# The third block of a normalised x: turned over by DMA in place of TensorE

## The reference

```
h = relu(layernorm(x))                                   # 1250 x 1024
s = sigmoid(h @ wenc.T + benc)                           # 1250 x 500
agg = segment_sum((s @ conv_weight)[src] * edge_weight, dst)
x = x + (agg + s @ lin_weight.T) @ wdec.T + bdec
h = relu(layernorm(x))
x = x + D^-1/2 (A + I) D^-1/2 (h @ W.T + b)              # A counts the edges src -> dst
```

## Time and profile before

| | |
|---|---|
| median of three runs | 471.36 us |
| the profiled execution | 471.27 us |
| its span | 469.5 us |
| TensorE busy | 461.0 us (98%) |
| VectorE busy | 317.4 us (68%) |
| ScalarE busy | 207.8 us (44%) |
| GpSimd busy | 44.0 us (9%) |
| transposing DMAs into h16T | 8, issued from 48.3 to 71.6 us |

### The profile page before, as it was taken

The page is one execution under the profiler, slowest core; times in us unless marked ns, Lnnn a source line. Parts: engine busy times, 40 slices in busy tenths (PEclk is TensorE's granted clock), DMA queues, the critical chain, the costliest instruction groups (busy, mean ns, idle before and its releaser), DMA issues.

```text
span 469.5 us, 9232 instructions
## 1 busy us (share of the span) xinstructions
PE 461.0 (98%) x3456; PEld 400.5 (85%) x3456; DVE 317.4 (68%) x596; ACT 207.8 (44%) x412; POOL 44.0 (9%) x60
## 2 busy tenths in 40 slices
PE   6999999999999999999999999999999999999997
PEld 5999999978888888889888878888889988888886
DVE  5999997777857851594668786929542467566652
ACT  6986797645541141222444444547442522222220
POOL 3522110000000000000000000465500000000000
PEclk8899999999999999999999999999999999999999
DMA  8820848482224570538530005161959315546542
GB/s 308 259 82 23 156 85 217 129 312 77 68 68 84 113 246 0 114 109 341 201 121 1 0 1 209 62 265 51 372 220 391 140 36 235 202 179 224 192 168 104
DMA packets 46111, 72.35 MB, mean 154 GB/s; under 512 B 25292, under 2 KB 34142, under 8 KB 44402
## 3 DMA queue, kind: packets, MB, share of 16 engines
q1 hardware_dynamic: 45746, 71.34, 45.4%
q0 software_dynamic: 320, 0.39, 0.4%
HBM read 44.33 MB, written 22.01 MB: 141 GB/s over the span
## 4 chain that ended last, share of the span: by engine, by line
PE 79%; DVE 9%; DMA 6%; ACT 3%; issue 2%; POOL 1%; SPq 0%; POOLq 0%; DVEq 0%; ACTq 0%
PE bank L1408 18%; PE bank L1424 18%; PE bank L1409 18%; PE bank L1410 18%; DVE weighted L1328 3%; DMA row_scratch<-dis 2%; PE bank L1521 2%; DMA raw<-adj_scratch 2%; DVE stats L1049 1%; PE bank L1566 1%; PE bank L1541 1%; DMA dis_row<-row_scratch 1%; PE bank L1523 1%; PE bank L1525 1%; DMA h<-x 1%
## 5 line engine op out<-in xcount | busy, mean ns | idle before, releaser
L1424 PE MATMUL bank<-a,h_hi 128*128 128x256 f16 (+3 forms) x400 | 85.5, 270 | 0.0
L1424 PE MATMUL bank<-a,h_lo 128*128 128x256 f16 (+3 forms) x400 | 85.5, 270 | 0.0
L1408 PE MATMUL bank<-right,left 128*128 128x512 f32 (+1 forms) x148 | 56.1, 379 | 0.0
L1409 PE MATMUL bank<-right,left 128*128 128x512 f32 (+1 forms) x148 | 55.9, 378 | 0.0
L1410 PE MATMUL bank<-right,left 128*128 128x512 f32 (+1 forms) x148 | 55.9, 378 | 0.0
L1393 DVE SCALAR_TENSOR_TENSOR x<-bank,dis_u,x 128x512 f32<-128x512 f32 (+2 forms) x37 | 26.7, 722 | 35.9 <-PE bank L1410 35.8
L1013 ACT CAST left<-zs 128x512 fp32r<-128x512 f32 x35 | 21.6, 624 | 61.3 <-PE bank L1410 61.2
L1408 PE MATMUL bank<-unit,g 128*128 128x500 f32 (+3 forms) x120 | 42.4, 354 | 0.4 <-DVE unit L1265 0.4
L1424 PEld LDWEIGHTS bank<-a,h_hi 128*128 128x128 f16 (+1 forms) x400 | 39.0, 98 | 4.1 <-issue 0.3
L1424 PEld LDWEIGHTS bank<-a,h_lo 128*128 128x128 f16 (+1 forms) x400 | 39.1, 98 | 3.7
L1410 PE MATMUL bank<-unit,g 128*128 128x500 f32 (+3 forms) x120 | 42.3, 352 | 0.0
(11 more groups left out here) (162 smaller groups left out, 1114.2 us busy)
## 6 DMA issues: line engine op xcount, KB each, us to landing
right_scratch<-right SPq DMA_DIRECT2D x5, 2048.0 KB, 8.1
right<-right_scratch SPq DMA_DIRECT2D x5, 2048.0 KB, 7.6
whole<-w SPq DMA_DIRECT2D x7, 1024.0 KB, 7.7
adj_scratch<-stage SPq DMA_DIRECT2D x50, 125.0 KB, 2.3
raw<-adj_scratch SPq DMA_DIRECT2D x2, 2500.0 KB, 8.9
h<-x SPq DMA_DIRECT2D x9, 512.0 KB, 6.0
x<-x SPq DMA_DIRECT2D x9, 512.0 KB, 6.8
out<-x SPq DMA_DIRECT2D x18, 256.0 KB
```

The source lines that it names most:

```text
L1408: pe.matmul(o, lhs[0], rhs[0], start=first, stop=False, skip_group_check=True)
L1409: pe.matmul(o, lhs[0], rhs[1], start=False, stop=False, skip_group_check=True)
L1424: ins = pe.matmul(o, h1[i][0:n, k, 128 * f:128 * (f + 1)], moving, start=(k == 0 and part == 0 and i == 0), stop=(k == T - 1 and part == p ...
```

## The change

Block 2 is turned over by DMA too. With `BY_DMA = 2` every place that asks for it treats tiles 4 and 5 as tiles 6 to 9 were treated: the factor in the scale, two activations in norm 4 and norm 5, splits, transposing DMAs, the copies L896 and L1157, and the sigmoids' scale. The 16 transposes, L899 and L1159 of this block are gone. The splits and the DMAs of tiles 4 and 5 come behind e(1,0), the copies behind e(1,2), each quarter's low part right behind its high part, and norm 6 after them. The DMAs of block 2 wait for `edges`, as it is now the first such block; those of block 3 now wait for block 2 to be copied; norm 6 writes `x16` after tile 4's DMAs, and norm 7 after tile 5's. In the order written out, the windows and hots 2 and 3 fall between e(1,2) and the copies of block 2; before, all of block 2 stood ahead of them.

```diff
-BY_DMA = 3
+BY_DMA = 2
...
     third, fourth, fifth = statistics(2), statistics(3), statistics(4)
     beside = {
-        (1, 0): turn(2), (1, 1): fourth, (1, 2): [("norm", 6)], (1, 3): [("norm", 7), ("split", 6), ("turn", 6)],
+        (1, 0): [("split", 4), ("turn", 4), ("split", 5), ("turn", 5)], (1, 1): fourth, (1, 2): both(turn(2)) + [("norm", 6)],
+        (1, 3): [("norm", 7), ("split", 6), ("turn", 6)],
         (2, 0): [("split", 7), ("turn", 7)] + fifth[:1], (2, 1): fifth[1:], (2, 2): both(turn(3)) + [("norm", 8)],
```

## The result

The changed kernel took 475.71 us (median of six, 474.98 to 477.26) against 471.3 us (471.05 to 471.7): a ratio of 1.0094, with a 95% interval of 1.0083 to 1.0105. The kernel became slower by 4.4 us, as forecast.

A forecast was written before the change was run, and what follows sets the result against it. TensorE's order of work was taken as the bound, with any wait put before it paid in full. Terms 1.14 - 1.67 + 0.85 + 1.6 + 2.0 + 0.2 + 0.3 = +4.4 us on 471.27 gave 475.7, range 472.4 to 479.0.

The forecast's parts named there:

- e(1,0): TensorE's encoder product of block 1, feature group 0: forecast +1.14 us late, behind norm 4's added activation.
- window 0: First ("win", w) step, on TensorE in block 1's products: forecast 0.53 us ahead, with the transposes' 1.67 us gone.
- e(2,0): Encoder product of block 2, feature group 0: forecast +1.9 us late, held by hots, the DMA and the first copies.
- e(2,1): Encoder product of block 2, feature group 1: forecast +3.9 us late, another +2.0 from ScalarE's queue behind the wait.
- e(2,2): Encoder product of block 2, feature group 2: forecast +4.1 us late, starting at 57.55 against 53.46.
- window 12: Later ("win", w) step on TensorE, waiting for ScalarE's stage: forecast +4.4 us late, another +0.3 from GpSimd's scale.
- the walk: Step-by-step forecast along the engines' orders: 475.7 us, its own range 474.7 to 476.9, chance 0.60.
- the landing of the last transfer: Tile 5's second transposing DMA: issued at 42.8, forecast to land 3.6 us later, at 46.4.
- The last hold: Norm 8 on ScalarE waits for GpSimd's scale: forecast start between 65.1 and 66.1, +3.9 to +4.9 us.
- ScalarE did not swallow it: Rival: ScalarE's 4.5 us free in 27 to 41 absorb the added 2.28 us: 469.6 us, chance 0.06.
- The quick transfer: Rival: tile 5 lands by 43.8 and norm 6 starts 2.6 us earlier: +1.8, 473.1 us, chance 0.12.
- The clock: Rival: TensorE's idle waits bring its granted clock down, costing another +2.5 us: 478.2 us, chance 0.14.

The follow-up runs named there:

- run 4: Changed kernel with norm 4 moved behind e(0,2), the product of block 0, feature group 2: 474.21 us, ratio 1.0069.
- run 5: Changed kernel with norm 4 moved behind the product of block 0, feature group 2, and norm 5 behind the step edges: 472.85 us, ratio 1.0036.
- run 6: Changed kernel with norm 4 as in run 4 and the splits and DMAs of tiles 4 and 5 ahead of the step edges: 470.7 us, ratio 0.9991.
- run 7: Changed kernel with norm 6 ahead of the copies of block 2: 477.47 us, ratio 1.013.
- run 8: Kernel of run 6 with norms 6 to 9 each one product later: 469.99 us, ratio 0.9974.
- run 10: Kernel of run 8 with the statistics of tile 8 ahead of split 6 on VectorE: 469.78 us, ratio 0.9963.
- run 11: Changed kernel with the splits and DMAs of tiles 4 and 5 ahead of the step edges, norm 4 not moved: 472.3 us, ratio 1.0017.
- run 12: Kernel of run 11 with 12 matmuls that nobody reads put into the step edges: 471.01 us, ratio 1.0009.
- run 1: Kernel before, block 2 still turned by TensorE, but norms 4 and 5 also write x16 (two activations for one): 473.6 us, ratio 1.0052.
- run 2: Changed kernel with the four DMAs of tiles 4 and 5 as plain copies, block 2 not turned over: 475.15 us, ratio 1.0088.
- run 3: Changed kernel with norm 5 moved behind the step edges: 473.87 us, ratio 1.0049.

## Why the prediction was right

Point by point, TensorE behind its own times of before, with the 0.77 us of the later start taken off:

| step | forecast | measured |
|---|---|---|
| e(1,0), behind norm 4's pair | +1.1 | +1.1 (32.19) |
| window 0, less the transposes | -0.5 | -0.7 (40.82) |
| e(2,0), behind the DMA | +1.9 | +2.8 (49.12) |
| e(2,1), behind norm 6 | +3.9 | +4.5 (54.82) |
| e(2,2) | +4.1 | +4.7 (58.97) |
| window 12, behind GpSimd's scale | +4.4 | +5.2 (70.95) |

Every hold of the walk is there, at its place and with the releaser named. One term was mis-sized: the landing of the last transfer. Its issue starts at 43.70 - 0.77 = 42.9, where the walk has it (42.8), but it lands 4.1 us later, not 3.6, and the copies begin at 47.94 - 0.77 = 47.2, not 46.4. That this issue took the queue 2.23 us is not in the sum, as the landing is counted from its start. The last hold is also past the walk's own +3.9 to +4.9: GpSimd's input leaves VectorE at 62.4 instead of 61.8 (with the 0.77 taken off), and GpSimd takes 4.05 us, towards the long end of 3.29 to 4.29. That nothing is given back behind window 12 holds: from there to the end of the span it is 404.5 us, before it was 404.6.

By the table the trace says 471.27 + 5.2 = 476.5 where the median is 475.7, so the hit on the median is better than the walk deserves, and partly luck. The profiled execution was the longest of six, and the others can't be taken apart. The landing does vary: in eight other profiles (runs 4 to 8 and 10 to 12) the last of the four landed in 3.2 or 3.3 us. In run 7, where splits and DMAs stand in the same places, that was 17.0 us behind the turning of the edges' fields, and 17.9 in the changed kernel's profile. A landing like that would take about 0.9 off the 5.2; that it was so in the median execution is not shown.

The rivals. ScalarE did not swallow it: run 1 costs 2.4 us by the activations alone. The quick transfer did not come, and run 2 shows why it could not: a plain copy too lands 3.8 us (median of four) behind its issue. In landing the two are alike (medians of 3.7 for the changed kernel's twelve and 3.8), and in issue they are not (5.46 to 6.49 us for four, and 3.43). The Trainium skill (Advanced Engine Details and Errata, section X-Bar Transpose (TRN2)) has the transposing DMA as fast as the plain one. By that rule the landing agrees and the queue's issue does not; as a rate no run here measures it. The clock did not fall from 27 us on in the changed kernel's profile, but it did in four others behind such waits (runs 2, 4, 7 and 11). So that the waits are short, which the prediction held against this rival, was no reason, and 0.14 was low. It is not what makes the kernel slower, though: one of the six timed executions had a mean clock of 1.000 over its span and took 475.12, 3.8 us over the kernel before. Whether a fall has a part in the 0.6 from there to the median remains open.

What caused the 4.4 us is shown by moving steps alone: 3.4 come back with the splits ahead of the edges (run 11), and 5.0 with norm 4 behind e(0,2) as well (run 6). Whether the sum's terms can be had one by one is not shown: runs 3 and 4 gave 1.8 and 1.5 us, both moves together in run 5 2.9, and the intervals do not tell 2.9 from 3.3. What is out is that the two moves take away the whole cost (469.7), as at each hold that goes the next one shows.

## What to carry to other kernels

When work moves from a full engine to one with room, ask where in the order of the receiving engine it lands, and what stands behind it there. Start the transfer early enough that the step which waits for it need not wait: here the same instructions cost +0.9% in one order and nothing in another, and -0.3% with the norms moved as well. Look for the engine that waits anyway (VectorE ahead of the edges' copies) and put the start of the transfer there. To move the waiting step back instead did not help here: behind norm 6 (run 7) it cost 1.8 us more, because the copies were themselves what TensorE needed next.

## What the runs showed of the hardware

- A single wait of TensorE of 1.5 us ahead of e(1,0), between stretches of full work, was followed by a fall of the clock in two profiles (0.83 and 0.61 in two stretches of 3 us in run 2, 0.78 and 0.65 in run 11) and not in four (1.00 in the changed kernel and in runs 1, 3 and 7). With the wait filled by twelve small matmuls the clock stayed at 1.00 in the one profile of run 12; that the filling did it is made likely by the mean clocks of all executions (1.000 in 9 of 12, against 2 of 12 without), not by this profile alone.
- Each of the four falls (runs 2, 4, 7 and 11) made TensorE's next stretch 1.5 to 1.9 us longer. Whether that is paid hangs on what TensorE waits for next: nothing of it in runs 2 and 4, where the copies or a stage came late anyway, all of it up to window 4 in run 7.
- The first three transposing DMAs took the queue 1.35, 1.33 and 1.40 us (from 39.44 on), the fourth 2.23, the longest of the kernel's twelve. It is not the fourth as such: the same four took 5.46 to 5.49 us in runs 3, 5, 6, 7, 10, 11 and 12, and 5.88 and 6.05 in runs 8 and 4. A late landing comes without a long issue too: in run 3 the last took the queue 1.35 us and landed after 4.4. Why was not tried.
